# One graph layer pair on one core: the output product put ahead of the sums of the new batch, and the steps after it moved one step later

## The reference, cut to what matters

```python
def _ngcf_conv(x, W1, W2, src, dst, n_nodes):
    deg_out = clip(segment_sum(ones, src), 1.0); deg_in = clip(segment_sum(ones, dst), 1.0)
    norm = rsqrt(deg_out[src] * deg_in[dst])
    msg = (x[src] @ W1 + x[src] * x[dst] @ W2) * norm[:, None]
    return x @ W1 + segment_sum(msg, dst, num_segments=n_nodes)
h = _ngcf_conv(x, W1_1, W2_1, src, dst, n)
h = relu(h)
h = _ngcf_conv(h, W1_2, W2_2, src, dst, n)
out = layernorm(x + h)
```

## Time and profile before

| | us |
|---|---|
| median of 3 runs | 1270.73 |
| lowest, highest | 1262.32, 1270.86 |
| the profiled execution | 1268.42 |
| its span, first to last instruction | 1266.8 |

### The profile page before, as it was taken

How to read it: one execution, slowest core, us unless ns; L and a number is a source line. 1 busy time by engine, 2 the same in 40 slices (tenths; PEclk the granted TensorE clock), 3 DMA queues, 4 the chain that set the end, 5 groups by cost and what they waited for, 6 DMA issues and landing times. The chain is left out here.

```text
span 1266.8 us, 33156 instructions
## 1 busy us (share of the span) xinstructions
PE 806.7 (64%) x12938; PEld 743.5 (59%) x12938; DVE 1003.4 (79%) x2582; ACT 715.0 (56%) x2723; POOL 810.5 (64%) x819
## 2 busy tenths in 40 slices
PE   1655367676767677766773566666766666766664
PEld 1554256566666666655662566666666665766664
DVE  8998578888898889888962678778878877788774
ACT  3000046665666566666662266667677667667665
POOL 6000677777777777777734777777777777667600
PEclk9999989988988898899885786888778788887885
DMA  6976112222222222222212133333333333333322
GB/s 130 199 220 280 42 37 52 53 52 52 52 52 52 53 52 52 57 51 58 53 40 58 27 68 68 77 76 76 69 69 76 77 77 77 67 67 80 67 45 48
DMA packets 148617, 93.63 MB, mean 74 GB/s; under 512 B 115880, under 2 KB 128616, under 8 KB 147948
## 3 DMA queue, kind: packets, MB, share of 16 engines
q1 hardware_dynamic: 122872, 64.77, 19.2%
q0 software_dynamic: 25472, 26.34, 12.0%
q10 hardware_dynamic: 116, 0.40, 0.1%
HBM read 52.75 MB, written 38.69 MB: 72 GB/s over the span
## 5 line engine op out<-in xcount | busy, mean ns | idle before, releaser
L591 POOL DMA_INDIRECT c_rows<-table,k_row_i x796 | 789.7, 992 | 395.7 <-issue 237.6
L608 PE MATMUL c_sum<-c_rest,c_sel 128*128 128x64 bf16 x3110 | 388.4, 215 | 0.0
L608 PE MATMUL c_sum<-c_lo,c_sel 128*128 128x64 bf16 x3110 | 388.2, 215 | 0.1
L608 PE MATMUL c_sum<-c_rows,c_sel 128*128 128x64 bf16 x1555 | 213.6, 224 | 201.5 <-DVE c_lo L746 181.9
L608 PEld LDWEIGHTS c_sum<-c_lo,c_sel 128*128 128x128 bf16 x3110 | 337.2, 113 | 0.2 <-issue 0.2
L608 PEld LDWEIGHTS c_sum<-c_rest,c_sel 128*128 128x128 bf16 x3110 | 336.6, 113 | 0.1
L608 PEld LDWEIGHTS c_sum<-c_rows,c_sel 128*128 128x128 bf16 x1555 | 180.2, 119 | 214.1 <-issue 214.1
L608 PE MATMUL c_sum<-c_yr,c_sel 128*128 128x64 bf16 x1555 | 174.1, 206 | 145.7 <-DVE c_lo L746 133.1
L608 PEld LDWEIGHTS c_sum<-c_yr,c_sel 128*128 128x128 bf16 x1555 | 156.9, 107 | 161.8 <-issue 161.8
L731 DVE TENSOR_SCALAR c_sel<-k_place,k_grid 128x512 bf16<-128x512 f16 (+2 forms) x796 | 234.8, 366 | 0.0
L660 ACT ACTIVATE c_sum<-c_sum,k_xh 128x64 f32<-128x64 f32 x784 | 172.1, 348 | 72.2 <-DVE c_sum L762 72.2
(11 more groups left out here) (134 smaller groups left out, 1074.8 us busy)
## 6 DMA issues: line engine op xcount, KB each, us to landing
c_rows<-table,k_row_i POOLq DMA_INDIRECT x796
table<-c_y SPq DMA_DIRECT2D x48, 256.0 KB
c_res<-in_x SPq DMA_DIRECT2D x48, 256.0 KB, 2.9
out<-c_y SPq DMA_DIRECT2D x48, 256.0 KB, 2.6
table<-k_xh SPq DMA_DIRECT2D x2, 3640.0 KB, 10.7
table<-k_xh SPq DMA_DIRECT2D x1, 3542.5 KB, 12.9
table<-k_xh SPq DMA_DIRECT2D x1, 1040.0 KB, 7.0
table<-k_xh SPq DMA_DIRECT2D x1, 520.0 KB, 5.5
```

The lines of the kernel that those rows point to most:

```text
L591: nc.gpsimd.indirect_dma_start(out=rows[:, b % RING, i], out_offset=None, in_=tables[l], in_offset=bass.IndirectOffsetOnAxis(ap=k.row_i[:, ...
L608: last = nc.tensor.matmul(p_sum[g % BANKS][:, t - GROUP[g][0], :], sel[:, b % 2, i, n * P:(n + 1) * P], part, start=first and q == 0, stop ...
```

## The change

What runs stays the same arithmetic; it is ordered otherwise, and a few steps change their engine.

- PE: `multiply` of group s - 3 stands first in step s, `add_up(s)` second.
- Stage 2: `centre` runs for group s - 4 in step s (was s - 3), at the end of DVE's step, `vary` (s - 5, as before in number) behind it; `square` moves from s - 4 to s - 5 and to the front of ACT's step; both halves of `deviate` and `normalize` move from s - 5 to s - 6; the store follows, and a stage has one step more.
- DVE: `cut(s)` stands ahead of `join`. ACT in stage 1: `relu` ahead of `add_own`.
- Count: stage 1 counts batches 0 to 46 but those with b mod 4 = 3 (batches 45 and 46 in steps 3 and 11); stage 2 counts the others and 48, 49, 50 (batches 47 to 50 in steps 5, 13, 21, 29). Stage 1 gives 14 chunks to stage 2 and neither counts in its last steps.
- Groups 48 and 49 alone: `scale`, the scaled output rows of stage 1 and `normalize` are one DVE instruction each in place of 4 (the last: 8 a pair) ACT instructions.

```diff
-COUNTED = [[b for b in range(BATCHES) if (b % 4 == 3) == l] for l in range(2)]
+COUNTED = [[b for b in range(48) if b % 4 != 3], [b for b in range(48) if b % 4 == 3] + [48, 49, 50]]
+COUNT_AT = [{b: b for b in COUNTED[0] if b < 45}, {b: b for b in COUNTED[1] if b < 45}]
+for l, late in enumerate(([45, 46], [47, 48, 49, 50])):
+    for i, b in enumerate(late):
+        COUNT_AT[l][3 + 8 * i if l == 0 else 5 + 8 * i] = b
+COUNTS = [[COUNT_AT[l][s] for s in sorted(COUNT_AT[l])] for l in range(2)]
+END_GROUPS = (GROUPS - 2, GROUPS - 1)
...
-        STEPS = range(BATCHES + 5)
+        STEPS = range(BATCHES + 6)
...
-                for g in ended(s - 2 - 2 * l):
+                for g in ended(s - 2 - 3 * l):
                     store(g)
...
             for s in STEPS:
+                for g in ended(s - 2):
+                    multiply(g)
                 if s < BATCHES:
                     add_up(s)
-                for g in ended(s - 2):
-                    multiply(g)
                 for g in ended(s - 1):
                     turn(g)
-                if s in COUNTED[l]:
-                    count(s)
+                if s in COUNT_AT[l]:
+                    count(COUNT_AT[l][s])
...
                 act.wait_ge(multiplied, g + 1)
+                if g in END_GROUPS:
+                    act.wait_ge(y_made, g + 1)
                 A(k.xh[:, a:b, 0:D], p_out[g % 2][:, 0:b - a, :], ACT.Relu)
+                if g in END_GROUPS:
+                    return
...
             for s in STEPS:
                 if l == 1:
                     for g in ended(s - 4):
+                        square(g)
+                    for g in ended(s - 5):
                         deviate(g)
                 for g in ended(s - 1):
-                    scale(g)
+                    if g not in END_GROUPS:
+                        scale(g)
+                if l == 0:
+                    for g in ended(s - 2):
+                        relu(g)
                 for g in ended(s):
                     add_own(g)
                 if l == 1:
-                    for g in ended(s - 4):
-                        normalize(g)
-                    for g in ended(s - 3):
-                        square(g)
-                else:
-                    for g in ended(s - 2):
-                        relu(g)
+                    for g in ended(s - 5):
+                        if g not in END_GROUPS:
+                            normalize(g)
                 for g in ended(s - 1):
                     turned_back(g)
...
+            def scale(g):
+                bank = p_sum[g % BANKS][:, 0:wide(g)]
+                dve.wait_ge(sums_made, g + 1)
+                V.tensor_tensor(bank, bank, norms(g), ALU.mult).then_inc(scaled_made, 1)
+            def scaled_rows(g):
+                w = wide(g)
+                dve.wait_ge(multiplied, g + 1)
+                dve.wait_ge(y_made, g)
+                done(dve, stored[g % 2], 16 * (g // 2))
+                V.scalar_tensor_tensor(y[:, g % 2, 0:w], p_out[g % 2][:, 0:w], 0.0, norms(g), ALU.max, ALU.mult).then_inc(y_made, 1)
+            def normalize(g):
+                w, j = wide(g), g % 4
+                dve.wait_ge(rstd_made, g + 1)
...
+                V.tensor_tensor(y[:, g % 2, 0:w], z[:, j, 0:w], rstd[:, j, 0:w].unsqueeze(2).to_broadcast([P, w, D]), ALU.mult).then_inc(y_made, 1)
...
             for s in STEPS:
-                if l == 1:
-                    for g in ended(s - 4):
-                        vary(g)
+                if s < BATCHES:
+                    cut(s)
                 for g in ended(s - 1):
                     join(g)
-                if s < BATCHES:
-                    cut(s)
+                    if g in END_GROUPS:
+                        scale(g)
                 if s + 1 < BATCHES:
                     select(s + 1)
                 if l == 1:
-                    for g in ended(s - 4):
+                    for g in ended(s - 5):
                         deviate(g)
+                        if g in END_GROUPS:
+                            normalize(g)
                 for g in ended(s - 1):
                     products(g)
-                if s in COUNTED[l]:
-                    hots(s)
-                if l == 1:
+                if s in COUNT_AT[l]:
+                    hots(COUNT_AT[l][s])
+                if l == 0:
                     for g in ended(s - 2):
+                        if g in END_GROUPS:
+                            scaled_rows(g)
+                else:
+                    for g in ended(s - 3):
                         centre(g)
+                    for g in ended(s - 4):
+                        vary(g)
```

More of the change, by code:

```diff
@@ L470 @@
 BANKS = 3
-COUNTED = [[b for b in range(BATCHES) if (b % 4 == 3) == l] for l in range(2)]
+COUNTED = [[b for b in range(48) if b % 4 != 3], [b for b in range(48) if b % 4 == 3] + [48, 49, 50]]
[5 more added lines that the diff above has]
+END_GROUPS = (GROUPS - 2, GROUPS - 1)
+assert sorted(COUNTS[0] + COUNTS[1]) == list(range(BATCHES))
 assert FIRST[-1] == CHUNKS
@@ L612, in count @@
             def count(b):
-                pe.wait_ge(hots_made, COUNTED[l].index(b) + 1)
+                pe.wait_ge(hots_made, COUNTS[l].index(b) + 1)
                 for i in range(BATCH[b]):
-                    last = nc.tensor.matmul(k.p_count[:, 0:TILES], hot_l[:, i], hot_t[:, i], start=l == 0 and b == COUNTED[0][0] and i == 0,
-                                            stop=l == 1 and b == COUNTED[1][-1] and i == BATCH[b] - 1, skip_group_check=True)
+                    last = nc.tensor.matmul(k.p_count[:, 0:TILES], hot_l[:, i], hot_t[:, i], start=l == 0 and b == COUNTS[0][0] and i == 0,
+                                            stop=l == 1 and b == COUNTS[1][-1] and i == BATCH[b] - 1, skip_group_check=True)
                 last.then_inc(counted, 1)
@@ L748, in hots @@
             def hots(b):
-                i = COUNTED[l].index(b)
+                i = COUNTS[l].index(b)
                 n, c = BATCH[b], FIRST[b]
@@ L762, in join, with norms @@
                 V.tensor_tensor(bank[:, 0:w], bank[:, 0:w], own[:, g % 2, 0:w], ALU.add).then_inc(sums_made, 1)
+            def norms(g):
+                a, b = GROUP[g]
+                return k.xh[:, a:b, D:ROW].to_broadcast([P, b - a, D])
+            def scale(g):
[11 more added lines that the diff above has]
+                dve.wait_ge(rstd_made, g + 1)
+                dve.wait_ge(y_made, g)
+                done(dve, stored[g % 2], 16 * (g // 2))
+                V.tensor_tensor(y[:, g % 2, 0:w], z[:, j, 0:w], rstd[:, j, 0:w].unsqueeze(2).to_broadcast([P, w, D]), ALU.mult).then_inc(y_made, 1)
             def products(g):
@@ L804, in verdict @@
             def verdict():
-                dve.wait_ge(counted, len(COUNTED[1]))
+                dve.wait_ge(counted, len(COUNTS[1]))
                 V.memset(differs[:, FULL_TILES:TILES], 0.0)
```

## The result

| | before | changed | ratio, 95% interval |
|---|---|---|---|
| median, first measurement | 1269.96 us | 1220.32 us (1215.92 to 1225.89) | 0.9625 (0.9581 to 0.9669) |
| median, measured again (run e5) | 1268.98 us | 1219.83 us (1218.1 to 1221.62) | 0.9605 (0.9567 to 0.9643) |
| profiled execution, first measurement | 1268.42 us, span 1266.8 | 1215.92 us, span 1213.7 | |

The changed kernel is 3.8% to 4.0% faster, 49.6 and 49.2 us by the medians.

What follows compares the result with a forecast made beforehand. Stage 1 was taken as bound by POOL's gathers, stage 2 by a circle of DVE and PE waits; 13.6 + 27.3 + 3.0 + 5.4 - 1.6 = 47.7 us off 1270.73 gives 1223.0, 8 in 10 from 1212 to 1240.

Steps and rivals of the forecast that it cites:

- POOL's waits less its slower pace, stage 2: Stage 2 until batch 48 lands: POOL's waits for PE's sums go, 13.6 us, less 1.6 for slower gathers.
- batch 48's lateness: Stage 2: batch 48's rows, cut 27.3 us after landing, would be cut as they land; 27.3 us gained.
- end of stage 1: After batch 48's gathers in stage 1: lighter last steps against the product ahead of the sums; gain 1.2 to 4.8, taken 3.0.
- end of stage 2: From batch 48's landing to the span's end: 39.7 us against 45.1, gain 5.4, range 2.4 to 8.4.
- body of stage 1: Stage 1's steps before its end, already set by the gathers at 10.42 us a batch: gain 0.
- The circle: Stage 2: DVE and PE wait in turn, 11.17 us a step; reordered, 9.55 remain around PE, under the gathers' 10.27.
- One of its signs of being wrong: Stage 2: the prediction is wrong if PE's sums wait for L668 through the product; no size given.
- The pace: POOL's gathers in stage 2, slowed by denser DVE from 1.283 to 1.287 us a chunk: a loss of 1.6 us.
- PE's clock: PE's clock in stage 2 would be 0.88 or more, from 0.82, since no pause exceeds about 1.5 us.
- Another closed wait: Stage 2: another wait closes at 10.3 to 11.2 us a step; chance 0.13 together with the slower-gathers rival, 1234 to 1258.
- the slower PE ring: Candidate for another closed wait: turn, copy, product, sums around PE take 11.0 us with the slow product; time 1258.
- rival 2: PE falls to its lower clock and in-order PE becomes the bound, 12.4 us a step, about 1320; chance 0.05.

Runs made afterwards that it cites:

- e5: The changed kernel measured again, no edit, beside the kernel before: 1219.83 us, ratio 0.9605.
- e6: The kernel before with only PE's order swapped, output product ahead of the sums: 1220.45 us, ratio 0.961.
- e7: The changed kernel with PE's order turned back, sums first and product second, later centre kept: 1226.04 us, ratio 0.965.
- e8: The changed kernel with sums first and `centre` one step earlier, reading the product of its own step: 1241.05 us, ratio 0.9779.
- e12: The changed kernel without the count of degrees (no hots, no count, no comparison of degrees), on a chip with PE's pauses: 1808.25 us, ratio 1.06.
- e2: The changed kernel with PE's order turned back, sums first, on a chip with PE's pauses: 1743.16 us, ratio 1.0336.
- e3: The changed kernel with the old sharing of the count between the stages, on a chip with PE's pauses: 1746.46 us, ratio 1.0326.
- e4: The changed kernel with groups 48 and 49 back on ACT tile by tile, on a chip with PE's pauses: 1740.17 us, ratio 1.0302.
- e9: The changed kernel with ACT's own rows ahead of `relu` in stage 1, on a chip with PE's pauses: 1764.37 us, ratio 1.0341.
- e1: The kernel before with only PE's product moved ahead of the sums, on a chip with PE's pauses: 1665.89 us, ratio 0.9866.
- e10: The changed kernel with the lags and other orders of before, keeping product first, new count, last groups on DVE; chip with PE's pauses: 1694.77 us, ratio 0.9939.

## Why the prediction was right

Predicted 1223.0 us, 47.7 us gained; measured 1220.32, 49.6 gained. By its steps, from the two profiled executions of the first measurement, which differ by 53.1 us in their spans (that of e5 differs from before by 49.2: by row -1.8, 2.5, 14.8, 26.5 and 7.1):

| term | predicted | measured |
|---|---|---|
| POOL's waits less its slower pace, stage 2 | 13.6 - 1.6 = 12.0 | 515.2 - 500.7 = 14.5 |
| batch 48's lateness | 27.3 | 29.8 - 3.8 = 26.0 |
| end of stage 1 | 3.0 | 37.3 - 34.8 = 2.5 |
| end of stage 2 | 5.4 | 45.1 - 38.1 = 7.0 |
| body of stage 1 | 0 | 509.2 - 506.3 = 2.9, scatter of POOL's pace |

*The circle.* Right, and shown from both sides: e6 opens it in the kernel before by PE's order alone, and from e7 to e8 one line of `centre` closes it again, with a lag of 10 us and a turn of 10.26 us with the parts named in the prediction. (The turn that the prediction printed, from `z` at 1195.13 to `z` at 1207.25, is a slow one of 12.12 us; 11.17 is the mean.) The prediction described the two edits as one opening; each of them would do, and together they bring little more in the body (gathers and lateness 503.7 us in e5, 503.3 in e7, 509.4 in e6).

One of its signs of being wrong did come: the sums now stand behind a product that waits for ACT's copy, 46.5 us in 30 waits from 760 to 1175, up to 1.9 us each. It did no harm: POOL never waited for the sums, and batch 48 was cut as it landed. PE had room for these waits, so the sign was badly chosen. DVE waits for landing rows in 25 of the some 40 steps of that stretch, 38.8 us, 1.0 us a step on average and not 1.3.

*The pace.* It took 1.287 us a chunk for stage 2; it was 500.7 / 391 = 1.281, as fast as in the kernel before once its waits are taken off (1.283). DVE at 369.8 / 415 = 89% of the stretch, against 80% in the earlier trace rows, did not slow the gathers. So the loss of 1.6 was wrong, and with it the reading that stage 1 is slower for its hots. The traces show what makes the difference. A gather is followed by the next after 0.30 us, so the pace is in the gathers' lengths, 0.94 us at best, and the long ones lie under DVE's `cut`. The changed kernel, one batch of stage 1, gathers on POOL and then DVE:

```profile
300.30 1.45 POOL L600 DMA_INDIRECT c_rows<-table,k_row_i  x1 [0.30 <-issue]
302.05 1.15 POOL L600 DMA_INDIRECT c_rows<-table,k_row_i  x1 [0.30 <-issue]
303.50 0.94 POOL L600 DMA_INDIRECT c_rows<-table,k_row_i  x1 [0.30 <-issue]
```

```profile
300.96 0.69 DVE L758 TENSOR_TENSOR c_rest<-c_yr 128x512 f32<-128x512 f32 x1
301.69 0.69 DVE L761 TENSOR_TENSOR c_lo<-c_rest 128x512 bf16<-128x512 f32 x1
302.30 0.69 DVE L777 TENSOR_TENSOR c_sum<-c_sum,c_own 128x512 f32<-128x512 f32 x1
302.90 2.18 DVE L746 TENSOR_SCALAR c_sel<-k_place,k_grid 128x512 bf16<-128x512 f16 x8
```

Taken over all 398 gathers of a stage, from the two engines' timelines:

| | gathers under `cut`: number, mean us | all others: number, mean us | all lengths over 0.94 us, summed |
|---|---|---|---|
| changed, stage 1 | 103, 1.085 | 295, 0.954 | 19.1 |
| changed, stage 2 | 93, 1.038 | 305, 0.956 | 14.0 |
| e5, stage 1 | 100, 1.132 | 298, 0.956 | 24.1 |
| e5, stage 2 | 93, 1.043 | 305, 0.952 | 13.3 |
| before, stage 1 | 98, 1.110 | 300, 0.958 | 22.1 |
| before, stage 2 | 75, 1.082 | 323, 0.963 | 18.1 |
| e12, without hots, stage 1 | 50, 1.250 | 348, 0.948 | 18.1 |

The last column gives both the difference between the stages (changed: 5.1 us, where the gathers differ by 5.6; e5: 10.8 and 10.6) and the scatter of stage 1 from one execution to the next (5.0 and 4.7). Stage 1's `cut` has one instruction more, the scaling into `yr`. Gathers with nothing but hots and selects beside them are 0.968 us in the changed kernel's stage 1 (132 of them), 3.7 us in all, and e12 has the long gathers without any hots. It isn't the place in the batch either: where the cut comes at ever other places of the batch (before, stage 2), 43 of 75 gathers under it take 1.0 us or more, against 27 of 323 others. No run changes `cut` alone, so this is a coincidence in time in every trace, and not an experiment. The Trainium skill, "SBUF — State Buffer", Who interferes with whom, has a DVE instruction in a two-port mode block GpSimd for its whole length. The trace shows no such block beside hots and selects, only the 3.7 us in all, and the difference between the stages does not come from them.

*The end of stage 1.* DVE's timeline of the changed kernel, batch 48's rows landing in stage 1 and the last `y` written:

```profile
638.85 0.73 DVE L755 TENSOR_TENSOR c_yr<-c_rows 128x512 f32<-128x512 f32 x1 [4.01 <-DMA c_rows<-table,k_row_i]
...
667.90 0.42 DVE L793 SCALAR_TENSOR_TENSOR c_y<-c_out,k_xh 128x256 f32<-128x256 f32 x1 [1.28 <-PE c_out L632]
```

The size was right (667.90 + 0.42 - 638.85 = 29.5 us, where the prediction's steps give 27.1 to 30.7), the reason in part wrong. The prediction named the product ahead of the sums as the cost and the lighter last steps as the gain. e6 and e7 show the reverse: product first gives 37.3 - 32.7 = 4.6 us alone, and 41.0 - 34.8 = 6.2 within the change; everything else together costs 34.8 - 32.7 = 2.1, where the own rows behind `relu` are the wait that shows (6.83 us). That 2.5 us came out where 3.0 was predicted is luck: a gain taken for a cost and a cost taken for a gain made up for each other. The step at fault is that the prediction weighed the product only against the sums of batch 50, and not against `relu`, the own rows and the next copy, all of which are queued behind the product. The 4.6 us compare executions on chips that may differ; the 6.2 are from one chip.

*The end of stage 2.* 39.7 us predicted from landing, 38.1 measured from the cut, which came as the rows landed. The gain was 7.0 us and not 5.4, and 5.8 of it come with PE's order alone (39.3 in e6); with the circle closed the same end takes 48.6 (e8). So the open circle gives it, more than the DVE instructions of the last groups. The landing itself took 1175.65 - 1171.87 - 1.40 = 2.4 us, not the 1.55 of stage 1.

*PE's clock.* Wrong. It was to be 0.88 or more in stage 2, and it is 0.85, after 0.82; in stage 1 it fell from 0.92 to 0.87. PE's order is what lowers it in stage 1: e6 has 0.87 there and e7, with the sums first, 0.92. The waits became shorter and came at more places: in stage 2 one of 3.6 us before the sums (141.8 us in all) gave way to waits before the product (46.5 us), the turn (21.1), the sums (20.6) and the count (19.4), up to 2.4 us each where the prediction had 1.5. The Trainium skill, "TensorE: Matmul & The Clock Gate", HAM oscillation, has waits between bursts bring the low clock; the trace agrees in direction in stage 2, where PE's waits went from 145.8 us in 443 to 107.6 in 415, and not in stage 1, where they went from 170.5 us to 137.7 and the clock fell all the same. Why is open. It cost nothing in the gathers, since POOL never waited for PE.

*The rivals.* Another closed wait and the slower PE ring did not come on the chips without the pauses. On the chips with PE's pauses rival 2's outcome did, by another mechanism: PE became the bound, and the changed kernel's neighbours with one edit (e2, e3, e4, e9) are slower than before, e3, e4 and e9 by 3.0% to 3.4% and the executions of e2 by 2.0% to 3.8%. The changed kernel itself was not run there. The profile of before, taken on a chip without the pauses, could not tell of it.

## What to carry to other kernels

Where two engines wait in turn although neither is full, write down the circle and look for the one hand-over that can be served from the step before: two moved lines on one engine's list did it here. An in-order engine should first do what others wait for; asked again for the last steps of stage 1, where the pipeline drains, the same question gave 4.6 to 6.2 us. Once the circle is shorter than the supply (gathers here), further opening brings little, and what remains is the supply's pace and the ends. Look into that pace as well: here its slow gathers lie under one step of another engine. And an order that is free on one chip need not be so on another: `cut` ahead of `join` does no visible harm where PE runs through, and costs some 58 us where it pauses.

## What the chips showed beside it

The kernel before took 1269 to 1270 us in two sets of runs and 1689 to 1705 us on three chips, where PE pauses: 586 to 612 times in the sums of an execution, together 463 to 558 us, at starts some 0.7 us apart where their neighbours are 0.03 to 0.05 us apart, with nothing in the profile that releases them. The pauses are not a fixed sum for a fixed list of PE instructions: 462.9 us in e1, 509.8 in e10, 558.0 in e9 with the same matrix products in another order, and 506.2 in e12 with fewer. What causes them stays open.
